# One ScalarE exponential per head in the softmax, in place of GpSimd's subtraction, one wide exponential and VectorE's sums

## Chip, cores and metric

The kernel runs on one core of one Trainium2 chip. The metric is the device time of one execution in microseconds (us). Most executions of one kernel agree within 0.3%.

## What is computed

There are 16 batches of 1024 rows of 512 numbers. Each row attends to the 64 context rows of its batch with 16 heads of 64 numbers each, and a feed-forward part follows. The shapes of the reference, cut to what matters here:

```python
x = x + _L0_xattn_ref(ctx_1024, _layernorm(x, axis=-1), fs, fs, ln1_w, ..., Wq, Wkv, Wout)
...
qk = jnp.einsum('bihd,bjhd->bhij', q, k) * attn_scale
attn = jax.nn.softmax(qk, axis=-1)          # over 64 context rows, for each of 16 heads
out = jnp.einsum('bhij,bjhd->bihd', attn, v)
...
x = x + tanh(layernorm(x) @ weight @ aux_weight1 @ aux_weight2 + bias)
```

## The kernel before

The program has a setup (up to about 150 us), in which weights are split into a high and a low part and multiplied together, and then a loop over 128 tiles of 128 rows. One pass of the loop is called a slot here. Slot t computes the scores and the softmax of tile t, the attention product of tile t-1, and the feed-forward part of tile t-2. Every 32-bit product is three passes on TensorE (PE): high times high, high times low, low times high.

Each engine has its own order of work, written out by hand in `slot_pe`, `slot_act`, `slot_dve`, `slot_pool` and `slot_sp`; each runs in order and waits on semaphores. In a slot PE does:

1. the scores of columns 0 to 511 (half q=0, heads 0 to 7) from xT (L154, L159), the transposes of tile t-2 (L702), the scores of half q=1;
2. the feed-forward product with x2T (L154, L159), which needs ScalarE's x2T_hi (L860) and VectorE's x2T_lo (L944);
3. the attention product of half 0: eight matmuls with pT_hi (L830), which wait for ScalarE's copy (L855), then four with pT_lo (L837), which wait for VectorE's L926; then the same for half 1.

The softmax of one half passes through four engines. VectorE (DVE) scales the scores and adds the bias (L901) and takes the maximum of each head (L906). GpSimd (POOL) subtracts it in two instructions of 256 columns (L994). ScalarE (ACT) takes the exponential of 512 columns in one instruction (L850). DVE sums each head (L912) and inverts the sums (L915). POOL multiplies by the inverse (L1001). SyncE writes the half to DRAM and reads it back rearranged (L752, L759), and in the next slot DVE transposes it (L921, p_turned) and ACT and DVE split it into pT_hi and pT_lo.

ACT's order in an ordinary slot is: x2T_hi, exp(0), pT_hi(0), xT_hi of the next tile (L719), exp(1), pT_hi(1), tanh (L884). DVE's is: x2 (L931), bn_stats, read scores 0, maximum(0), transpose(0), x2T_lo, read scores 1, maximum(1), inverse_sums(0), pT_lo(0), transpose(1), inverse_sums(1), ln1_stats with pT_lo(1) inside it, hid (L977).

Once per batch two slots carry more. Slot m=7 (the last of a batch) folds the next batch's keys into M: 16 pieces on PE (L614, L615), each of which ACT rounds (L632, L633) and DVE and POOL complete (L645, L648, L655), through four PSUM banks; its ACT order is exp(1), pieces 0 and 1, `bias_copy` (L684), pT_hi(1), more pieces. PE does not start the attention product of half 0 there before `s_bs`, the end of `bias_copy`. Slot m=0 folds the values: ACT's `v_prepare_act` (L574) and DVE's `diag_lo` (L557) write bd, then PE makes eight pieces of N from it (L154, L159). There are 15 slots of either kind in the loop, 97 ordinary slots with an attention product, and one slot t=0.

Of the kernel before, what the change touches and what calls it, by code (L numbers as in the profile page):

```python
# [41 lines left out]
ALU = mybir.AluOpType  # L42
ACT = mybir.ActivationFunctionType
AX_XY = mybir.AxisListType.XY

P = 128
# [3 lines left out]
CTX, H, DH = 64, 16, 64  # L50
# [10 lines left out]
def build(nc, x, x_turned, ctx_rows, fs_cols, ln1_w, ln1_b, ln2_w, ln2_b, wqT, wkv, wout, ffn_wT, aux1T, aux2,  # L61
# [7 lines left out]
    with ExitStack() as ctx:  # L69
        def sb(name, cols, dt=F32):  # L70
            return ctx.enter_context(nc.sbuf_tensor(name, [P, cols], dt))

        def sem(name):
            return ctx.enter_context(nc.semaphore(name))
# [26 lines left out]
        mv1, mv2, mv_w = sb("mv1", 2), sb("mv2", 2), sb("mv_w", 8)  # L101
        var1, var2 = sb("var1", 1), sb("var2", 1)
        rs1, rs2 = sb("rs1", 1), sb("rs2", 1)
        row_max = [sb(f"row_max{i}", H) for i in range(2)]
        row_sum = [sb(f"row_sum{i}", H) for i in range(2)]
        row_inv = [sb(f"row_inv{i}", 2 * H) for i in range(2)]

# [19 lines left out]
        S = [take(INNER) for _ in range(2)]  # L127
        xT = [take(D) for _ in range(2)]
        hid = take(D)
        bias = take(INNER)  # L130
# [12 lines left out]
        def at_least(eng, s, n):  # L143

            if not isinstance(n, int) or n > 0:
                eng.wait_ge(s, n)
# [331 lines left out]
        two = lambda name: [sem(f"{name}{i}") for i in range(2)]  # L478
# [5 lines left out]
        s_xT = two("s_xT")  # L484
        s_xTh, s_xTl = sem("s_xTh"), sem("s_xTl")
        s_x2T, s_x2Th, s_x2Tl = sem("s_x2T"), sem("s_x2Th"), sem("s_x2Tl")
        s_sc, s_sb, s_mx, s_sub, s_ex = two("s_sc"), two("s_sb"), two("s_mx"), two("s_sub"), two("s_ex")
        s_sum, s_inv, s_p = two("s_sum"), two("s_inv"), two("s_p")
        s_pw, s_pr = two("s_pw"), two("s_pr")
        s_pt, s_pTh, s_pTl = two("s_pt"), two("s_pTh"), two("s_pTl")  # L490
        s_o, s_x2, s_f, s_fb, s_th, s_y = (sem(n) for n in ("s_o", "s_x2", "s_f", "s_fb", "s_th", "s_y"))
# [8 lines left out]
        J2 = CTX // 2  # L500
        heads = lambda a: a.rearrange("p (h s k j) -> p h k s j", h=2, s=2, j=J2)
        half_of = lambda a, q: a[:, q * BANK:(q + 1) * BANK]
        H2 = H // 2
# [66 lines left out]
        def v_prepare_act(act, b):  # L570
            act.wait_ge(s_vin, 16 * b + 16)
            act.wait_ge(s_m, 16 * b + 16)
            for half in range(2):
                last = act.copy(diag(0, half), dense(kvf, half))  # L574
            last.then_inc(s_vh, 1)
# [92 lines left out]
        def fold_hi(act, b8, cs, produced, done, dst):  # L668
            for c in cs:
                act.wait_ge(produced, b8 + c + 1)  # L670
                act.copy(dst(c), fold_ps[c % 4][:]).then_inc(done, 1)
# [44 lines left out]
        def xT_split_hi(act, u, r):  # L716
            act.wait_ge(s_xT[r], 8 * (u - r) + 16)
            at_least(act, s_sc[1], u)
            act.copy(xT_hi[:], xT[r]).then_inc(s_xTh, 1)  # L719
# [7 lines left out]
        def parts(t, m):  # L727

            known = isinstance(t, int)
            return dict(scores=not known or t < T, following=not known or t + 1 < T,  # L730
                        attn=not known or 1 <= t <= T, chain=not known or t >= 2,
                        fold_m=m == 7 and (not known or t + 1 < T), fold_n=m == 0 and (not known or t < T),
                        more=not known or t + TPB < T)

        def ended(t, m):


            return not isinstance(t, int) or t >= 2
# [104 lines left out]
        def slot_act(act, t, m):  # L843
            has = parts(t, m)
            first = isinstance(t, int) and t == 0

            def exp(q):
                act.wait_ge(s_sub[q], t + 1)
                s = half_of(S[m % 2], q)
                act.activation(s, s, ACT.Exp).then_inc(s_ex[q], 1)  # L850

            def pT_hi_part(q):
                at_least(act, s_o, t - 1)
                act.wait_ge(s_pt[q], t)
                act.copy(half_of(pT_hi, q), half_of(p_turned, q)).then_inc(s_pTh[q], 1)  # L855

            if has["chain"]:
                act.wait_ge(s_x2T, t - 1)
                at_least(act, s_f, t - 2)
                act.copy(x2T_hi[:], x2T_ps[:]).then_inc(s_x2Th, 1)  # L860
            if has["scores"]:
                exp(0)
            if has["attn"]:
                pT_hi_part(0)
            if has["following"]:
                xT_split_hi(act, t + 1, (m + 1) % 2)
            if first:
                fold_hi(act, t, range(6), s_n, s_nh, N_fold[2])
            if has["scores"]:
                exp(1)  # L870
            if has["fold_m"]:
                m_act(act, t + 1, range(2))
                bias_copy(act, t + 1)
            if has["attn"]:
                pT_hi_part(1)
            if has["fold_n"] and not first:
                v_prepare_act(act, t // 8)
            if has["more"] and m == 4:
                k_prepare_act(act, (t + 4) // 8)
            if has["fold_m"]:  # L880
                m_act(act, t + 1, range(2, 10))
            if ended(t, m):
                act.wait_ge(s_fb, t - 1)
                act.activation(hid, hid, ACT.Tanh).then_inc(s_th, 1)  # L884
            if has["fold_m"]:
                m_act(act, t + 1, range(10, 16))
            if has["fold_n"]:
                fold_hi(act, t, range(6 * first, 8), s_n, s_nh, N_fold[2])

        def slot_dve(dve, t, m):  # L890
# [12 lines left out]

            def maximum(q):
                dve.wait_ge(s_sb[q], t + 1)
                dve.tensor_reduce(row_max[m % 2][:, q * H2:(q + 1) * H2], heads(half_of(S[m % 2], q)), AX_XY,  # L906
                                  ALU.max).then_inc(s_mx[q], 1)

            def inverse_sums(q):
                hs = slice(q * H2, (q + 1) * H2)  # L910
                dve.wait_ge(s_ex[q], t + 1)
                dve.tensor_reduce(row_sum[m % 2][:, hs], heads(half_of(S[m % 2], q)), AX_XY, ALU.add).then_inc(s_sum[q], 1)  # L912
                dve.wait_ge(s_sum[q], t + 1)
                sums = row_sum[m % 2][:, hs].rearrange("p (h k) -> p h k", h=2).unsqueeze(2).to_broadcast([P, 2, 2, 4])
                dve.reciprocal(row_inv[m % 2][:, q * H:(q + 1) * H].rearrange("p (h s k) -> p h s k", h=2, s=2),  # L915
                               sums).then_inc(s_inv[q], 1)
# [69 lines left out]
        def slot_pool(pool, t, m):  # L986
            has = parts(t, m)

            def subtract_maximum(q):
                pool.wait_ge(s_mx[q], t + 1)  # L990
                for h in range(2):
                    s = half_of(S[m % 2], q)[:, h * 256:(h + 1) * 256].rearrange("p (s k j) -> p s k j", s=2, j=J2)
                    row = row_max[m % 2][:, q * H2 + 4 * h:q * H2 + 4 * h + 4].unsqueeze(1).unsqueeze(3)
                    last = pool.tensor_tensor(s, s, row.to_broadcast([P, 2, 4, J2]), ALU.subtract)  # L994
                last.then_inc(s_sub[q], 1)

            def normalise(q):
                pool.wait_ge(s_inv[q], t + 1)
                s = half_of(S[m % 2], q).rearrange("p (c j) -> p c j", j=J2)
                inv = row_inv[m % 2][:, q * H:(q + 1) * H].unsqueeze(2).to_broadcast([P, H, J2])  # L1000
                pool.tensor_tensor(s, s, inv, ALU.mult).then_inc(s_p[q], 1)  # L1001

            if has["chain"]:
                pool.wait_ge(s_var2, t - 1)
                at_least(pool, s_fb, t - 2)
                pool.tensor_tensor(rs2[:], var2[:], minus_half[:], ALU.pow).then_inc(s_rs2, 1)  # L1006
            if has["scores"]:
                subtract_maximum(0)
                subtract_maximum(1)
                normalise(0)  # L1010
            if has["fold_m"]:
                m_pool(pool, t + 1, range(1))
            if has["scores"]:
                normalise(1)
            if has["fold_m"]:
                m_pool(pool, t + 1, range(1, 3))
            if has["following"]:
                xT_split_lo(pool, t + 1, (m + 1) % 2)
                pow1(pool, t + 1)
            if has["fold_m"]:  # L1020
                m_pool(pool, t + 1, range(3, 5))
            if ended(t, m):
                pool.wait_ge(s_th, t - 1)
                pool.tensor_tensor(xr[(m - 2) % RING], xr[(m - 2) % RING], hid, ALU.add).then_inc(s_y, 1)
            if has["fold_m"]:
                m_pool(pool, t + 1, range(5, 8))
            if has["more"] and m == 3:
                k_prepare_pool(pool, (t + 5) // 8)
            if has["more"] and m == 4:
                ku_split_lo(pool, (t + 4) // 8)  # L1030
# [86 lines left out]
```

## Time and profile before

| | |
|---|---|
| median of 3 runs | 2230.62 us (2225.62 to 2231.32) |
| the profiled execution, its own time | 2226.84 us |
| its span | 2224.8 us |
| granted TensorE clock, mean | 0.995 of full |
| busy | PE 98%, DVE 82%, POOL 60%, ACT 37% of the span |

Busy shares are averages over the whole span. Whether an engine is in the way is read from what waits for it, and when in a slot.

### The profile page before, as it was taken

To read this page: it belongs to the slowest core of one execution; us is meant where nothing else is said; L and a number is where in the kernel's file an instruction comes from. 1 tells how busy PE (TensorE), PEld (TensorE's weight loads), DVE (VectorE), ACT (ScalarE), POOL (GpSimd) and SP (SyncE) were. 2 spreads that over 40 slices of the span, in tenths; PEclk is the share of its full clock that TensorE was granted. 3 is DMA by queue.
4 is the path that set the end of the run, shared out by engine and by line. 5 is a ranking of instruction groups with operands and counts; after the bars stand their busy time and mean duration, and the time that the engine had idled before them with its cause. 6 is when DMAs were issued, how large, how long until landed. Compare 5 with 4: busy or idle time off the path is not lost.

```text
span 2224.8 us, 34423 instructions
## 1 busy us (share of the span) xinstructions
PE 2169.7 (98%) x10176; PEld 1795.2 (81%) x10176; DVE 1819.1 (82%) x3388; ACT 829.1 (37%) x1623; POOL 1342.2 (60%) x1490
## 2 busy tenths in 40 slices
PE   6999999999999999999999999999999999999998
PEld 5877888888888888888888888888888888878886
DVE  6658888888888888887888888788888888888886
ACT  3353333434333343433334343333434343333422
POOL 4326656575765657575565757556575766657564
PEclk9999999999999999999999999999999999999999
DMA  6434434243433434343342434334243433424342
GB/s 208 158 103 133 121 109 137 95 141 99 127 113 114 131 94 141 99 128 113 115 130 94 141 99 128 112 115 130 94 141 99 129 111 119 131 94 140 96 133 86
DMA packets 284652, 267.19 MB, mean 120 GB/s; under 512 B 61008, under 2 KB 192336, under 8 KB 284624
## 3 DMA queue, kind: packets, MB, share of 16 engines
q1 hardware_dynamic: 284624, 266.84, 38.3%
q8 instruction: 14, 0.23, 0.0%
q14 instruction: 14, 0.11, 0.0%
HBM read 157.68 MB, written 109.05 MB: 120 GB/s over the span
## 4 chain that ended last, share of the span: by engine, by line
PE 81%; DVE 10%; issue 4%; POOL 2%; ACT 1%; DMA 0%; ACTq 0%; SPq 0%; DVEq 0%; POOLq 0%
PE bank L154 34%; PE bank L830 17%; PE bank L159 17%; PE bank L837 9%; PE bank L702 3%; PE bank L614 2%; DVE bd L557 2%; DVE area L645 1%; DVE area L901 1%; DVE row_max L906 1%; DVE bn L691 1%; POOL area L994 1%; DVE p_turned L921 1%; DVE row_sum L912 1%; DVE pT_lo L926 1%
## 5 line engine op out<-in xcount | busy, mean ns | idle before, releaser
L994 POOL TENSOR_TENSOR area<-area,row_max 128x256 f32<-128x256 f32 x512 | 303.9, 615 | 240.9 <-DVE row_max L906 236.2
L154 PE MATMUL bank<-M_hi,xT_hi 128*128 128x512 f32 x1024 | 410.9, 401 | 0.0
L830 PE MATMUL bank<-N_hi,pT_hi 128*128 128x512 f32 x1024 | 402.2, 393 | 0.2
L154 PE MATMUL bank<-M_lo,xT_hi 128*128 128x512 f32 x1024 | 400.7, 391 | 0.0
L830 PE MATMUL bank<-N_lo,pT_hi 128*128 128x512 f32 x1024 | 400.2, 391 | 0.0
L1001 POOL TENSOR_TENSOR area<-area,row_inv 128x512 f32<-128x512 f32 x256 | 326.7, 1276 | 97.2 <-DVE row_inv L915 97.2
L901 DVE SCALAR_TENSOR_TENSOR area<-bank,rs,area 128x512 f32<-128x512 f32 x256 | 192.1, 751 | 176.3 <-PE bank L159 174.2
L850 ACT ACTIVATE area<-area 128x512 f32<-128x512 f32 x256 | 162.1, 633 | 427.1 <-POOL area L994 427.0
L1006 POOL TENSOR_TENSOR rs<-var,minus_half 128x1 f32<-128x1 f32 x128 | 70.5, 551 | 347.8 <-DVE var L698 347.8
L159 PE MATMUL bank<-M_hi,xT_lo 128*128 128x512 f32 x1024 | 274.5, 390 | 3.9 <-POOL xT_lo L724 3.9
L837 PE MATMUL bank<-N_hi,pT_lo 128*128 128x512 f32 x1024 | 276.0, 391 | 1.2 <-DVE pT_lo L926 1.2
L926 DVE TENSOR_TENSOR pT_lo<-p_turned,pT_hi 128x512 fp32r<-128x512 f32 x256 | 262.7, 1026 | 5.4 <-ACT pT_hi L855 1.0
L860 ACT CAST x2T_hi<-bank 128x512 fp32r<-128x512 f32 x128 | 75.2, 587 | 413.7 <-PE bank L702 413.7
L159 PEld LDWEIGHTS bank<-M_hi,xT_lo 128*128 128x128 f32 x1024 | 192.2, 188 | 44.7 <-POOL xT_lo L724 4.3
L830 PEld LDWEIGHTS bank<-N_hi,pT_hi 128*128 128x128 f32 x1024 | 193.4, 189 | 40.3 <-issue 0.5
L830 PEld LDWEIGHTS bank<-N_lo,pT_hi 128*128 128x128 f32 x1024 | 193.4, 189 | 39.4
L154 PEld LDWEIGHTS bank<-M_lo,xT_hi 128*128 128x128 f32 x1024 | 193.3, 189 | 37.1
L154 PEld LDWEIGHTS bank<-M_hi,xT_hi 128*128 128x128 f32 x1024 | 193.0, 188 | 36.2
L837 PEld LDWEIGHTS bank<-N_hi,pT_lo 128*128 128x128 f32 x1024 | 189.8, 188 | 39.5 <-DVE pT_lo L926 1.8
L724 POOL TENSOR_TENSOR xT_lo<-area,xT_hi 128x512 fp32r<-128x512 f32 x127 | 214.6, 1689 | 0.0
L154 PE MATMUL bank<-W_hi,x2T_hi 128*128 128x512 f32 x512 | 199.4, 389 | 1.4 <-ACT x2T_hi L860 1.4
L154 PE MATMUL bank<-W_lo,x2T_hi 128*128 128x512 f32 x512 | 199.2, 389 | 0.0
(127 smaller groups left out, 4123.8 us busy)
## 6 DMA issues: line engine op xcount, KB each, us to landing
p_scratch<-area SPq DMA_DIRECT2D x256, 256.0 KB, 2.0
p_moved<-p_scratch SPq DMA_DIRECT2D x1024, 64.0 KB, 2.1
area<-x_dram SPq DMA_DIRECT2D x128, 256.0 KB, 2.7
area<-x_turned_dram SPq DMA_DIRECT2D x128, 256.0 KB, 2.8
y_dram<-area SPq DMA_DIRECT2D x128, 256.0 KB, 2.1
kv_scratch<-area SPq DMA_DIRECT2D x32, 256.0 KB, 2.4
area<-kv_scratch SPq DMA_DIRECT2D x32, 256.0 KB, 3.6
area<-wkv_dram SPq DMA_DIRECT2D x5, 512.0 KB, 4.5
```

What stands on the lines that cost most here:

```text
L154: mm = eng.matmul(ps, sh, mv, start=(n == 0), stop=False)
L159: mm = eng.matmul(ps, sl, mh, start=False, stop=(k == len(pairs) - 1))
L724: eng.tensor_tensor(xT_lo[:], xT[r], xT_hi[:].bitcast(F32), ALU.subtract).then_inc(s_xTl, 1)
L830: pe.matmul(O_ps[:], pT_hi[:, k * P:(k + 1) * P], n_cols(mv, k), start=(k == 0 and mv is N_hi), stop=False)
L837: mm = pe.matmul(O_ps[:], pT_lo[:, k * P:(k + 1) * P], n_cols(N_hi, k), start=False, stop=(k == 7))
L850: act.activation(s, s, ACT.Exp).then_inc(s_ex[q], 1)
L860: act.copy(x2T_hi[:], x2T_ps[:]).then_inc(s_x2Th, 1)
L901: dve.scalar_tensor_tensor(out=half_of(S[m % 2], q), in0=S_ps[q][:], scalar=rs1[:, 0:1], in1=half_of(bias, q), op0=ALU.mult, op1=ALU.add). ...
L926: dve.tensor_tensor(half_of(pT_lo, q), half_of(p_turned, q), half_of(pT_hi, q).bitcast(F32), ALU.subtract).then_inc(s_pTl[q], 1)
L994: last = pool.tensor_tensor(s, s, row.to_broadcast([P, 2, 4, J2]), ALU.subtract)
L1001: pool.tensor_tensor(s, s, inv, ALU.mult).then_inc(s_p[q], 1)
L1006: pool.tensor_tensor(rs2[:], var2[:], minus_half[:], ALU.pow).then_inc(s_rs2, 1)
```

## The change

The maximum is stored negated. ACT then takes it as its bias, one column for each head, and gives the sum of the exponentials as its accumulated output: eight instructions of 128x64 (2 runs of 32 columns) for each half in place of one of 128x512. GpSimd's subtractions and VectorE's sums are no longer there. Two waits that guard the reuse of `neg_max` and `row_sum` two tiles later are added (`s_inv` on ACT, `s_ex` on DVE); the semaphores `s_sub` and `s_sum` are gone.

```diff
@@ slot_act
             def exp(q):
-                act.wait_ge(s_sub[q], t + 1)
-                s = half_of(S[m % 2], q)
-                act.activation(s, s, ACT.Exp).then_inc(s_ex[q], 1)
+                act.wait_ge(s_mx[q], t + 1)
+                at_least(act, s_inv[q], t - 1)
+                by_head = heads(half_of(S[m % 2], q))
+                for h in range(2):
+                    for k in range(4):
+                        i = q * H2 + 4 * h + k
+                        e = act.activation(by_head[:, h, k], by_head[:, h, k], ACT.Exp, bias=neg_max[m % 2][:, i:i + 1],
+                                           accum_out=row_sum[m % 2][:, i:i + 1])
+                e.then_inc(s_ex[q], 1)
@@ slot_dve
             def maximum(q):
                 dve.wait_ge(s_sb[q], t + 1)
-                dve.tensor_reduce(row_max[m % 2][:, q * H2:(q + 1) * H2], heads(half_of(S[m % 2], q)), AX_XY,
-                                  ALU.max).then_inc(s_mx[q], 1)
+                at_least(dve, s_ex[q], t - 1)
+                dve.tensor_reduce(neg_max[m % 2][:, q * H2:(q + 1) * H2], heads(half_of(S[m % 2], q)), AX_XY,
+                                  ALU.max, negate=True).then_inc(s_mx[q], 1)
 
             def inverse_sums(q):
                 hs = slice(q * H2, (q + 1) * H2)
                 dve.wait_ge(s_ex[q], t + 1)
-                dve.tensor_reduce(row_sum[m % 2][:, hs], heads(half_of(S[m % 2], q)), AX_XY, ALU.add).then_inc(s_sum[q], 1)
-                dve.wait_ge(s_sum[q], t + 1)
@@ slot_pool
-            def subtract_maximum(q):
-                pool.wait_ge(s_mx[q], t + 1)
-                for h in range(2):
-                    s = half_of(S[m % 2], q)[:, h * 256:(h + 1) * 256].rearrange("p (s k j) -> p s k j", s=2, j=J2)
-                    row = row_max[m % 2][:, q * H2 + 4 * h:q * H2 + 4 * h + 4].unsqueeze(1).unsqueeze(3)
-                    last = pool.tensor_tensor(s, s, row.to_broadcast([P, 2, 4, J2]), ALU.subtract)
-                last.then_inc(s_sub[q], 1)
-
...
             if has["scores"]:
-                subtract_maximum(0)
-                subtract_maximum(1)
                 normalise(0)
```

On ACT in a slot m=7, before the change (L719 is xT_hi, L850 exp(1), L632 and L633 the pieces 0 and 1 of M, L684 the four copies of `bias_copy`, L855 is pT_hi(1); `area` holds the scores, `bank` is PSUM):

```order
L719 CAST xT_hi<-area 128x512
L850 ACTIVATE area<-area 128x512
L627 ISA
L632 COPY area<-bank 128x256
L633 CAST M_hi<-bank 128x2x4x32
L627 REGISTER_ALU
L633 CAST M_hi<-bank 128x2x4x32
L684 COPY area<-bank 128x4x2x32 x4
L855 CAST pT_hi<-p_turned 128x512
```

The same place in the changed kernel:

```order
L719 CAST xT_hi<-area 128x512
L854 ACTIVATE area,row_sum<-area,neg_max 128x2x32 x8
L627 ISA
L632 COPY area<-bank 128x256
L633 CAST M_hi<-bank 128x2x4x32
L627 REGISTER_ALU
L633 CAST M_hi<-bank 128x2x4x32
L684 COPY area<-bank 128x4x2x32 x4
L861 CAST pT_hi<-p_turned 128x512
```

Nothing changes its place; the pieces of M, `bias_copy` and pT_hi(1) stand behind eight instructions where they stood behind one.

On DVE in an ordinary slot, before (L906 is the maximum of half 1, L912 and L915 are the sums and their inverses, L926 is pT_lo, L921 the transpose of half 1):

```order
L906 TENSOR_REDUCE row_max<-area 128x8
L912 TENSOR_REDUCE row_sum<-area 128x8
L915 RECIPROCAL row_inv<-row_sum 128x16
L926 TENSOR_TENSOR pT_lo<-p_turned,pT_hi 128x512
L921 STREAM_TRANSPOSE p_turned<-p_moved 128x512
L912 TENSOR_REDUCE row_sum<-area 128x8
L915 RECIPROCAL row_inv<-row_sum 128x16
L691 BN_STATS bn<-area 128x6
```

And in the changed kernel:

```order
L913 TENSOR_REDUCE neg_max<-area 128x8
L920 RECIPROCAL row_inv<-row_sum 128x16
L931 TENSOR_TENSOR pT_lo<-p_turned,pT_hi 128x512
L926 STREAM_TRANSPOSE p_turned<-p_moved 128x512
L920 RECIPROCAL row_inv<-row_sum 128x16
L691 BN_STATS bn<-area 128x6
```

The two sums are gone from their places; the inverses still wait for the exponentials of their half, and what follows on DVE stands behind them as before.

## Rows read from the trace of the kernel before

**Rows 1.** The page, busy time, share of the span and instructions of each engine.

```profile
PE 2169.7 (98%) x10176; PEld 1795.2 (81%) x10176; DVE 1819.1 (82%) x3388; ACT 829.1 (37%) x1623; POOL 1342.2 (60%) x1490
```

**Rows 2.** Windows: slots m=6, 7, 0. Length, then PE, PEld, DVE, ACT, POOL busy.

```profile
880.25:894.32 14.07, 14.07 (x66) 11.65 (x65) 11.42 (x21) 4.14 (x8) 8.95 (x11) 1.00 0.43 132
894.32:918.50 24.18, 23.38 (x134) 19.91 (x133) 19.25 (x43) 12.52 (x36) 14.87 (x19) 1.00 0.36 106
918.50:939.12 20.62, 19.84 (x90) 16.08 (x89) 18.06 (x32) 9.08 (x16) 10.12 (x11) 1.00 0.26 89
```

**Rows 3.** Timeline of PE, slot m=6: attention product, halves 0 and 1. Start, length.

```profile
888.88 0.39 PE L830 MATMUL bank<-N_hi,pT_hi 128*128 128x512 f32 x1
...
891.60 0.39 PE L830 MATMUL bank<-N_hi,pT_hi 128*128 128x512 f32 x1
```

**Rows 4.** Timeline of POOL and DVE, slot m=6.

```profile
884.93 1.19 POOL L994 TENSOR_TENSOR area<-area,row_max 128x256 f32<-128x256 f32 x2
...
884.17 0.68 DVE L906 TENSOR_REDUCE row_max<-area 128x8 f32<-128x512 f32 x1
...
890.86 0.25 DVE L915 RECIPROCAL row_inv<-row_sum 128x16 f32<-128x16 f32 x1
...
891.70 1.09 DVE L926 TENSOR_TENSOR pT_lo<-p_turned,pT_hi 128x512 fp32r<-128x512 f32 x1
```

**Rows 5.** Timeline of ACT, slot m=6.

```profile
886.15 0.63 ACT L850 ACTIVATE area<-area 128x512 f32<-128x512 f32 x1 [1.95 <-POOL area L994]
886.68 0.60 ACT L855 CAST pT_hi<-p_turned 128x512 fp32r<-128x512 f32 x1
887.20 0.62 ACT L719 CAST xT_hi<-area 128x512 fp32r<-128x512 f32 x1
...
890.35 0.62 ACT L855 CAST pT_hi<-p_turned 128x512 fp32r<-128x512 f32 x1 [0.59 <-DVE p_turned L921]
```

**Rows 6.** Groups by line: count, then busy, mean ns of one, idle before.

```profile
L850 ACT ACTIVATE area<-area 128x512 f32<-128x512 f32 x256 | 162.1, 633 | 427.1 <-POOL area L994 427.0
...
L860 ACT CAST x2T_hi<-bank 128x512 fp32r<-128x512 f32 x128 | 75.2, 587 | 413.7 <-PE bank L702 413.7
...
L632 ACT COPY area<-bank 128x256 f32<-128x256 f32 x128 | 47.8, 373 | 64.3 <-POOL M_lo L655 37.3 <-PE bank L615 26.7
```

**Rows 7.** Groups by line, DVE.

```profile
L901 DVE SCALAR_TENSOR_TENSOR area<-bank,rs,area 128x512 f32<-128x512 f32 x256 | 192.1, 751 | 176.3 <-PE bank L159 174.2
...
L931 DVE TENSOR_TENSOR area<-bank,area 128x512 f32<-128x512 f32 x128 | 88.3, 689 | 65.8 <-PE bank L837 65.4
...
L698 DVE TENSOR_SCALAR var<-mv 128x1 f32<-128x1 f32 x256 | 39.5, 154 | 10.1
...
L392 DVE DVE_READ_ACCUMULATOR area<-area 128x1 f32 x6 | 0.5, 81 | 0.0
```

**Rows 8.** Timelines of ACT, DVE and PE, slot m=7.

```profile
903.73 0.35 ACT L632 COPY area<-bank 128x256 f32<-128x256 f32 x1
...
910.28 0.76 DVE L645 TENSOR_TENSOR area<-bank,M_hi 128x256 f32<-128x256 f32 x2
...
906.12 0.45 PE L830 MATMUL bank<-N_hi,pT_hi 128*128 128x512 f32 x1
...
910.83 0.38 PE L614 MATMUL bank<-bd,Wq_hi 128*128 128x256 f32 x1 [0.33 <-DVE area L645]
```

**Rows 9.** Timelines of DVE and PE, slot m=0.

```profile
922.59 0.68 DVE L906 TENSOR_REDUCE row_max<-area 128x8 f32<-128x512 f32 x1
...
929.96 1.09 DVE L926 TENSOR_TENSOR pT_lo<-p_turned,pT_hi 128x512 fp32r<-128x512 f32 x1
...
933.52 0.50 PE L154 MATMUL bank<-Wo_hi,bd 128*128 128x512 f32 x1 [0.78 <-DVE bd L557]
```

**Rows 10.** Windows around a fall of the clock (PEclk is third from last).

```profile
1039.80:1043.20 3.40, 2.70 (x16) 2.26 (x17) 3.30 (x10) 1.54 (x4) 3.14 (x5) 0.94 0.48 128
1043.20:1046.60 3.40, 3.40 (x11) 2.74 (x11) 1.57 (x4) 0.92 (x3) 2.67 (x4) 0.56 0.15 59
```

More of the change, by code:

```diff
@@ L103, in build @@
         rs1, rs2 = sb("rs1", 1), sb("rs2", 1)
-        row_max = [sb(f"row_max{i}", H) for i in range(2)]
+        neg_max = [sb(f"neg_max{i}", H) for i in range(2)]
         row_sum = [sb(f"row_sum{i}", H) for i in range(2)]
@@ L486, in build @@
         s_x2T, s_x2Th, s_x2Tl = sem("s_x2T"), sem("s_x2Th"), sem("s_x2Tl")
-        s_sc, s_sb, s_mx, s_sub, s_ex = two("s_sc"), two("s_sb"), two("s_mx"), two("s_sub"), two("s_ex")
-        s_sum, s_inv, s_p = two("s_sum"), two("s_inv"), two("s_p")
+        s_sc, s_sb, s_mx, s_ex = two("s_sc"), two("s_sb"), two("s_mx"), two("s_ex")
+        s_inv, s_p = two("s_inv"), two("s_p")
         s_pw, s_pr = two("s_pw"), two("s_pr")
```

## The prediction, made before the changed kernel had run

> **What bounds the kernel now.** I read the page's busy times first: PE is busy for 98% of the span, ACT for 37% [rows 1]. So PE sets the time, and the two engines that are relieved, POOL and DVE, can give back only what PE idles for them. The windows by slot show how much that is. An ordinary slot lasts 14.07 us and PE is busy in all of it; PE idles 24.18 - 23.38 = 0.80 us in slot m=7 and 20.62 - 19.84 = 0.78 us in slot m=0 [rows 2]. With 15 batches in the loop, a perfect relief is worth at most 15 x 1.58 = 24 us.
>
> What the change can cost is read from the slack of the work that PE waits for. I count in us from the start of the slot (880.25 for m=6), and read the timelines. PE begins the attention product of half 0 at 8.63 and that of half 1 at 11.35 [rows 3]. They need ACT's pT_hi(0) and pT_hi(1), which stand in ACT's queue behind exp(0) and exp(1). Before, pT_hi(1) begins at 10.10 and ends at 10.72 [rows 5], 0.63 early. No engine's busy share shows this deadline.
>
> **The change, part by part.** Let e be the time from the start of one small exponential to that of the next, its accumulator read included.
>
> *The new time of pT_hi(1), ordinary slot.* The maximum of half 0 ends at 884.17 + 0.68 - 880.25 = 4.60, and its user on POOL begins 0.08 later, at 4.68 [rows 4]. ACT can now begin there. On ACT the copies behind an instruction start 0.53 and 0.52 after it [rows 5], though they last 0.60 and more. So exp(0) holds ACT until 4.68 + 8e, pT_hi(0) and xT_hi until 0.52 x 2 later, exp(1) until 5.72 + 16e; pT_hi(1) ends 0.62 later, and I give 0.07 for the signal to PE (about that from DVE to POOL). PE then has it at 6.41 + 16e. Against 11.35 the stall is **16e - 4.94** where that is positive: the threshold is e = 0.309 us. pT_hi(0) comes at 4.68 + 8e + 0.62 + 0.07 and meets 8.63 up to e = 0.41, so it is not the first to be late.
>
> *What is late next.* DVE's second inverse can start at 5.89 + 16e; the exponential before it ends at 5.82 + 16e, the overlap of 0.10 included. pT_lo(1) starts 891.70 - 890.86 = 0.84 after that inverse and lasts up to 1.09 [rows 4]: 7.82 + 16e. PE wants it eight matmuls (eight of the twelve that fill the 2.72 from half to half, 1.81) after pT_hi(1), at 8.22 + 16e. It keeps 0.3 of slack at any e. The two removed sums lie on DVE, which in an ordinary slot nobody waits for, so they are priced at nothing; so are POOL's subtractions, whose cover is PE's full 14.07 us. If POOL or DVE were the bound they would be worth 2.4 and 1.3 us a slot. The two added waits are for what happened two tiles ago, long past; nothing queues behind them. The DMAs behind POOL's multiplication are issued from the same places.
>
> *The size of e.* No row of the trace shows a 128x64 exponential, a bias column or an accumulator read on ACT. A 512-column exponential takes 633 ns; 587 and 373 ns for 512 and 256 columns from PSUM give 0.836 ns a column [rows 6]. That leaves 205 ns fixed, and 258 ns for 64 columns; less the 0.10 by which the next one overlaps it [rows 5], 0.158. Below this e cannot fall. For the bias column the nearest rows are DVE's: 751 ns with a scalar column against 689 ns without, 62 ns. For the accumulator read it is DVE's own, 81 ns, where a small DVE instruction takes 154 ns [rows 7]. Taken as they stand they give e = 0.301; scaled by the fixed parts of the two engines (205 to 154) they are 83 and 108 ns and e = 0.349. I take **0.33**, between the two. The upper end is that each extra costs a whole fixed part: 0.158 + 2 x 0.205 = 0.568.
>
> The Trainium skill, ScalarE: Activation LUTs, under What ACT_TABLE_LOAD costs, states about 280 ns + 0.833 ns a column with a bias column, and 93 ns of overlap back to back; for 64 columns that is an estimate of 0.240 for the exponential alone, against my 0.220 to 0.241, and it has no price for the accumulator read. This trace has 633 ns for 512 columns without the column, where its rule gives 613. With its 0.240 and my scaled read e would be 0.348, and the sum about 2336 us.
>
> *The sum.* With 16e = 5.28:
> - 97 ordinary slots, 5.28 - 4.94 = 0.34 each: 33 us.
> - Slot m=7: ACT reaches piece 0 of M at 5.72 + 16e; before, it did at 903.73 - 894.32 = 9.41 [rows 8]. So it is 16e - 3.69 = 1.59 late, because before ACT stood idle between its copies and exp(1). Everything behind it moves: `bias_copy` and with it `s_bs`, for which PE holds back half 0 (906.12, no slack but some 0.3); piece 0 of M_hi, then DVE's piece 0, its transpose, pT_hi(1) on ACT, pieces 2 and 3, and DVE's piece 4, for which PE was already waiting (DVE 910.28, PE 910.83 after 0.33 idle [rows 8]). DVE does its steps between without a break, so the 1.6 arrives at PE whole: 15 x 1.6 = 24 us. The saved sum of half 1 does not help there, as DVE waits for ACT at that point.
> - Slot m=0: exp(0) can start at 922.59 + 0.68 + 0.08 - 918.50 = 4.85. That is 0.17 later than in the ordinary slot, so pT_lo(1) starts at 5.89 + 16e + 0.17 + 0.84 = 6.90 + 16e = 12.18, against 929.96 - 918.50 = 11.46; DVE's two writes of bd follow without a gap, and PE was waiting for them already (0.78 idle before 933.52) [rows 9]. So 0.72 more, the slot's own stall included: 15 x 0.72 = 11 us.
>
> Together 68 us. Against the profiled execution's own 2226.8 us that is 2295; that execution was 3.8 us under the median shown, so for a median I say 2230.6 + 68 = **2299 us**, 3% slower. The sum is steep: above the threshold each nanosecond of e is 16 x 127 slots, 2.0 us.
>
> **The rivals.**
> - *The forecast, and the clock falls too.* The trace shows one stretch of 3.4 us with a mean granted clock of 0.56, behind a stretch in which PE was busy for 2.70 of 3.40 us, in a slot m=7 [rows 10]. That is all but wholly the lower of its two levels, 1.2 GHz. Such a stretch loses 3.4 x 0.44 = 1.5 us. Slot m=7 gets 1.6 us more idle time; if this always brings the fall, 15 x 1.5 = 22 us are added: 2321 us. For it: the place is the same. Against it: slots m=0 idle 0.78 at a time at clock 1.00 [rows 2], and the new idle time is spread over several waits.
> - *The accumulator read is a whole instruction on ACT*, 0.205 unoverlapped, with the column at 62 ns: e = 0.425, 16e = 6.80. The ordinary slots stall 1.86, m=7 3.1, m=0 2.2: 180 + 47 + 34 = 261 us, 2492 us. For it: it needs the sum that the exponential before it has just finished. Against it: DVE's costs half of a small instruction of its engine. The skill speaks for this side too: the same page, under Rules for kernel authors, budgets 0.3 us + 0.83 ns a column for every exponential with a bias column, 0.353 for 64 and with DVE's read 0.434, about 2507 us. The rows here show ACT starting the next instruction 0.10 before the last ends [rows 5], which that budget leaves out. At the upper end, e = 0.568, it would be 403 + 82 + 68 = 553 us, 2784 us.
> - *The small exponentials are covered*, e between 0.23 and 0.309: no stall in ordinary slots, only the fold slots pay. At e = 0.301, 16e = 4.82: 17 us for m=7 and 4 for m=0, 2252 us. It is DVE's prices unscaled.
> - *Faster: the relief decides.* Below e = 0.228, where 16e = 3.65, ACT reaches the pieces of M earlier than before and DVE, without 1.3 us of sums, finishes them earlier. At e = 0.158 nearly all of PE's idle time could go: up to 24 us, 2207 us. It needs both extras to be free, or nearly.
>
> **How the numbers follow.** The chances: the forecast 0.40, with the clock 0.15, the dear read 0.22, covered 0.13, faster 0.10. The time is that of the forecast, whose own range, with e from 0.301 to 0.349, is 2252 to 2336. From 2245 to 2490 lie nearly all of the first, second and fourth case and about half of the third, so 8 in 10. 0.3% is 6.7 us, about what a measurement of this kernel can tell from no change: this corresponds to e from 0.21 to 0.255. Most of the last case is beyond it, and a little of the covered one within it: faster 0.07, same 0.07, slower 0.86.
>
> **What would show each step.** The exponentials' group: 2048 instructions and as many accumulator reads, with a start-to-start of 0.33; ACT's busy share up from 37% to about 58% (829 - 162 + 2048 x 0.33 = 1343 us). In an ordinary slot exp(0) starting 4.68 into it and a wait of about 0.3 us of PE L830 for ACT's pT_hi at half 1, none at half 0; the slot 14.4 us. In slot m=7 PE waiting for `bias_copy` and DVE's pieces, the slot near 25.8 us; m=0 near 21.3. No new wait for POOL or a DMA. The prediction is wrong if e is far from 0.33, which is its weakest number, or if PE waits at another place than pT_hi(1).

## The result and the profile after

The changed kernel takes 2311.74 us (median of 4, 2309.98 to 2312.57) against 2229.75 us (4 runs, 2225.62 to 2231.32): ratio 1.037, 95% interval 1.0352 to 1.0388. That is 82 us slower, where 68 were forecast, and 13 us over the predicted 2299.

The page of the changed kernel, its busy times, which answer to [rows 1], then the groups of its longest-running new instructions:

```profile
PE 2214.7 (96%) x10176; PEld 1792.5 (78%) x10176; DVE 1716.7 (74%) x3132; ACT 1349.6 (58%) x5463; POOL 985.5 (43%) x978
...
L854 ACT ACTIVATE area<-area,neg_max 128x64 f32<-128x64 f32 x2048 | 683.5, 335 | 103.3 <-DVE neg_max L913 103.3
...
L854 ACT ACTIVATION_READ_ACCUMULATOR area<-area,neg_max 128x1 f32 x2048 | 383.1, 187 | 0.0
```

ACT went from 37% to 58%, DVE and POOL lost 102 and 357 us of work, and the kernel is slower: none of the four shares says so. What says it is the windows of the same three kinds of slot as in [rows 2], an ordinary one, m=7 and m=0:

```profile
914.35:928.88 14.53, 14.36 (x65) 11.58 (x64) 10.63 (x19) 8.20 (x38) 6.17 (x7) 1.00 0.41 128
928.88:954.67 25.79, 24.02 (x133) 20.16 (x132) 18.34 (x41) 16.76 (x66) 12.18 (x15) 1.00 0.30 99
954.67:975.97 21.30, 20.14 (x89) 16.01 (x88) 17.34 (x30) 13.12 (x46) 7.34 (x7) 1.00 0.26 87
```

The lengths were 14.07, 24.18 and 20.62; they grew by 0.46, 1.61 and 0.68. Where PE waits in the changed kernel, from the view of waits (total, times, longest):

```profile
PE bank L830 <- ACT pT_hi L861: 24.4, 112, 1.3
PE bank L614 <- DVE area L645: 22.5, 45, 0.7
PE bank L154 <- DVE bd L557: 12.5, 15, 0.9
```

The first row is the new one: 112 waits of the attention product for pT_hi, all of them at half 1. One ordinary slot shows it. It starts at 990.50 with PE's first score matmul. The timelines of DVE, ACT and PE:

```profile
994.43 0.69 DVE L913 TENSOR_REDUCE neg_max<-area 128x8 f32<-128x512 f32 x1
...
995.15 0.35 ACT L854 ACTIVATE area<-area,neg_max 128x64 f32<-128x64 f32 x1 [0.71 <-DVE neg_max L913]
995.41 0.19 ACT L854 ACTIVATION_READ_ACCUMULATOR area<-area,neg_max 128x1 f32 x1
995.50 0.34 ACT L854 ACTIVATE area<-area,neg_max 128x64 f32<-128x64 f32 x1
...
999.84 0.70 DVE L926 STREAM_TRANSPOSE p_turned<-p_moved 128x512 f32<-128x512 f32 x1
...
1001.43 0.19 ACT L854 ACTIVATION_READ_ACCUMULATOR area<-area,neg_max 128x1 f32 x1
1001.52 0.60 ACT L861 CAST pT_hi<-p_turned 128x512 fp32r<-128x512 f32 x1
...
1000.94 1.07 PE L837 MATMUL bank<-N_hi,pT_lo 128*128 128x512 f32 x4
1002.18 0.50 PE L830 MATMUL bank<-N_hi,pT_hi 128*128 128x512 f32 x1 [0.17 <-ACT pT_hi L861]
1002.52 0.39 PE L830 MATMUL bank<-N_lo,pT_hi 128*128 128x512 f32 x1
```

Read it against the prediction's walk. exp(0) starts 4.65 into the slot (4.68 forecast). The pair of an exponential and its read repeats every 0.33 us: the read starts 0.24 behind its exponential, the next exponential 0.09 behind the read. pT_hi(1) starts at 11.02, where the walk with e = 0.333 gives 5.72 + 16 x 0.333 = 11.05, right behind the last read. Its input, DVE's transpose, had been done for 1.0 us (at 1000.54), so it is ACT's own queue that held it. PE has pT_hi(1) at 11.68, where it wanted it at 11.35. That is 0.33 of stall by the start times; the row's own 0.17 of idle is less because the profile models the end of the matmul before. The other 0.13 of the slot's 0.46 was not in the sum: after the wait the first matmul runs 0.50, and the second starts 0.34 behind it instead of 0.23.

### The profile page after: what moved, and what is told of

It reads as the page before. It is cut to its first block, busy times and chain, and to the rows that moved or that the text cites. A ratio compares the mean times of both kernels' runs of the same rounds, so it can differ in the third digit from the quotient of the medians.

```text
span 2309.9 us, 37999 instructions
## 1 busy us (share of the span) xinstructions
PE 2214.7 (96%) x10176; PEld 1792.5 (78%) x10176; DVE 1716.7 (74%) x3132; ACT 1349.6 (58%) x5463; POOL 985.5 (43%) x978
## 4 chain that ended last, share of the span: by engine, by line
PE 40%; ACT 36%; DVE 12%; issue 10%; POOL 1%; DMA 0%; DVEq 0%; ACTq 0%; SPq 0%; POOLq 0%
ACT area L854 27%; PE bank L154 15%; PE bank L830 11%; PE bank L159 8%; ACT pT_hi L861 5%; PE bank L837 5%; DVE neg_max L913 4%; ACT xT_hi L719 3%; PE bank L614 2%; DVE bd L557 1%; DVE area L645 1%; DVE mv L695 1%; DVE area L907 1%; DVE bn L691 1%; PE bank L615 0%
## 5 line engine op out<-in xcount | busy, mean ns | idle before, releaser
L854 ACT ACTIVATE area<-area,neg_max 128x64 f32<-128x64 f32 x2048 | 683.5, 335 | 103.3 <-DVE neg_max L913 103.3
L998 POOL TENSOR_TENSOR area<-area,row_inv 128x512 f32<-128x512 f32 x256 | 269.1, 1051 | 726.5 <-DVE row_inv L920 726.5
L830 PE MATMUL bank<-N_hi,pT_hi 128*128 128x512 f32 x1024 | 417.8, 408 | 26.3 <-ACT pT_hi L861 24.4
L854 ACT ACTIVATION_READ_ACCUMULATOR area<-area,neg_max 128x1 f32 x2048 | 383.1, 187 | 0.0
L931 DVE TENSOR_TENSOR pT_lo<-p_turned,pT_hi 128x512 fp32r<-128x512 f32 x256 | 307.7, 1202 | 43.8 <-ACT pT_hi L861 39.4
L890 ACT ACTIVATE area<-area 128x512 f32<-128x512 f32 x128 | 80.9, 632 | 270.0 <-DVE area L982 270.0
```

Of the source, the lines that this page charges most:

```text
L830: pe.matmul(O_ps[:], pT_hi[:, k * P:(k + 1) * P], n_cols(mv, k), start=(k == 0 and mv is N_hi), stop=False)
L854: e = act.activation(by_head[:, h, k], by_head[:, h, k], ACT.Exp, bias=neg_max[m % 2][:, i:i + 1], accum_out=row_sum[m % 2][:, i:i + 1])
L931: dve.tensor_tensor(half_of(pT_lo, q), half_of(p_turned, q), half_of(pT_hi, q).bitcast(F32), ALU.subtract).then_inc(s_pTl[q], 1)
```

## The experiments

The theory is the prediction's: PE waits because pT_hi(1), and in the fold slots other work, stands on ACT behind sixteen small exponentials. The rivals are that each small instruction costs in proportion, that ACT simply has too much work, or that the loss lies elsewhere (DVE's inverses, POOL, the DMAs). Slot lengths below are windows from one slot's first score matmul to the next. Runs 1 to 4 were on one chip, 5 to 8 on a second and 9 and 10 on a third; each group has its own runs of the kernel before (medians 2228.95, 2230.14 and 2228.89 us).

### 1. One more small exponential in each half

```diff
                 by_head = heads(half_of(S[m % 2], q))
+                spare = idle_tile[:, (2 * (m % 2) + q) * 65:(2 * (m % 2) + q + 1) * 65]
+                act.activation(spare[:, 0:64]..., idle_in..., ACT.Exp,
+                               bias=neg_max[m % 2][:, q * H2:q * H2 + 1], accum_out=spare[:, 64:65])
                 for h in range(2):
```

> The changed kernel with a ninth exponential (128x64, bias column, accumulated output) ahead of the eight of each half, on spare tiles; nothing reads it. Theory (the start-to-start time of the small exponentials, 0.333 us, times their number sets when pT_hi(1) reaches PE): 2 x 0.333 = 0.67 us more in every slot with an attention product, ordinary slots 14.53 to 15.20, m=7 and m=0 the same 0.67 longer, 127 x 0.67 = 85 us, 2397 us. Rival (ACT's order is not what PE waits for; the loss comes from DVE's later inverses or from POOL and the DMAs behind them and has slack): clearly less than 85 us, ordinary slots under 14.9.

Measured: 2394.02 us, ratio 1.0743 (1.0725 to 1.0761), 82 us over the changed kernel. The windows:

```profile
940.74:955.97 15.23, 14.43 (x65) 11.58 (x64) 10.70 (x19) 8.88 (x42) 6.18 (x7) 1.00 0.38 122
955.97:982.43 26.46, 24.93 (x133) 21.24 (x132) 18.38 (x41) 17.25 (x70) 12.18 (x15) 0.94 0.32 97
982.43:1004.39 21.96, 20.22 (x90) 15.95 (x88) 17.33 (x30) 13.79 (x50) 7.33 (x7) 1.00 0.25 84
```

Each kind of slot is 0.66 to 0.70 longer than in the changed kernel, where 0.67 was expected. Time on ACT ahead of pT_hi(1) goes one for one into the time of the kernel, in all three kinds. The rival that expects slack falls. The second row has a fall of the clock in it (0.94) and is yet no longer than its like; the last section comes back to it.

### 2. The bias column without the sums

```diff
-                        e = act.activation(..., ACT.Exp, bias=neg_max[m % 2][:, i:i + 1],
-                                           accum_out=row_sum[m % 2][:, i:i + 1])
+                        e = act.activation(..., ACT.Exp, bias=neg_max[m % 2][:, i:i + 1])
@@ inverse_sums
                 dve.wait_ge(s_ex[q], t + 1)
+                dve.tensor_reduce(row_sum[m % 2][:, hs], heads(half_of(S[m % 2], q)), AX_XY, ALU.add).then_inc(s_sum[q], 1)
+                dve.wait_ge(s_sum[q], t + 1)
```

> The changed kernel without the accumulated outputs: sixteen small exponentials with the bias column, DVE's two sums back in their old places, POOL's subtractions still gone. Theory: without its accumulator read an exponential takes 0.24 start to start (the ACTIVATE to its read in the trace of the changed kernel), 16 x 0.24 = 3.84, pT_hi(1) reaches PE at 6.41 + 3.84 = 10.25 of the slot and is covered until 11.35; ordinary slots 14.07, m=7 later by 3.84 - 3.69 = 0.15, sum 2 us: 2232 us, same as before within what can be told. Rival (it is the number of ACT instructions and their waits, not the reads, that costs): ordinary slots stay above 14.3, 2265 us or more.

Measured: 2251.23 us, ratio 1.0107 (1.009 to 1.0123), 19 us more than expected. The windows of an ordinary slot, of m=7, and of the slots m=2 and m=3, then ACT's exp(0) in an ordinary slot:

```profile
890.06:904.13 14.07, 14.07 (x65) 11.66 (x64) 11.17 (x21) 6.83 (x21) 6.46 (x7) 1.00 0.42 131
904.13:928.57 24.44, 23.45 (x133) 19.98 (x132) 18.95 (x43) 15.03 (x49) 12.25 (x14) 1.00 0.33 104
963.17:977.58 14.41, 14.40 (x66) 11.52 (x65) 11.99 (x21) 6.28 (x21) 5.60 (x6) 1.00 0.37 123
977.58:992.28 14.70, 14.31 (x65) 11.59 (x64) 11.09 (x21) 6.77 (x22) 6.53 (x8) 1.00 0.47 145
```

```profile
894.72 2.02 ACT L854 ACTIVATE area<-area,neg_max 128x64 f32<-128x64 f32 x8 [0.71 <-DVE neg_max L912]
896.65 0.60 ACT L860 CAST pT_hi<-p_turned 128x512 fp32r<-128x512 f32 x1
```

The ordinary slot is back at 14.07 with sixteen small exponentials in it: their number is not what costs. Eight of them hold ACT for 1.93 us, 0.24 each, and sixteen stay under the threshold of 4.94. Slot m=7 is 0.26 over before, where 0.15 was expected. The miss is elsewhere. Slot m=2, the last of one pass of the program's loop, is 0.33 longer in every batch, and slot m=3, the first of the next pass, 0.5 to 1.4 longer in the 14 passes that follow another one: some 16 us together. (Expectation 6 below divides this as 1.0 and 0.2; it had set the end of m=2 0.55 too late.) This is DVE at the start of such a slot m=3, which begins at 325.21:

```profile
327.75 0.69 DVE L937 TENSOR_TENSOR area<-bank,area 128x512 f32<-128x512 f32 x1 [2.64 <-issue]
```

DVE's first instruction of the new pass starts 2.54 us into the slot, where it is 0.20 in slots m=3 of the kernel before. DVE is idle for 2.64 us before it, and the release is given as "issue": it waited for nothing that the profile shows. Runs 6, 9 and 10 take this up.

### 3. The same work, with pT_hi(1) ahead of exp(1)

```diff
@@ slot_act
                 pT_hi_part(0)
+                pT_hi_part(1)
...
                 bias_copy(act, t + 1)
-            if has["attn"]:
-                pT_hi_part(1)
@@ slot_dve (behind x2T_lo; then in place of the second transpose and inverse)
+            if has["attn"]:
+                turn_p(1)
...
-                turn_p(1)
-            if has["scores"]:
-                inverse_sums(1)
+                pT_lo_part(1)
...
-                ln1_stats(dve, t + 1, (m + 1) % RING, (lambda: pT_lo_part(1)) if has["attn"] else None)
+                ln1_stats(dve, t + 1, (m + 1) % RING, (lambda: inverse_sums(1)) if has["scores"] else None)
```

> The changed kernel with the same instructions in another order: on ACT pT_hi(1) ahead of xT_hi and exp(1), on DVE the second transpose behind x2T_lo, pT_lo(1) ahead of ln1_stats, the second inverse inside ln1_stats. Theory (PE waits because pT_hi(1) stands behind exp(1)): ordinary slots 14.07 again, though ACT does as much as in the changed kernel; m=0 about 0.25 over its 20.61 of before; m=7 still late, as the pieces of M and bias_copy stand behind exp(1): 1.4 over 24.20. 2230 + 25 = 2254 us. Rival (ACT has too much work in a slot, wherever it stands): slots stay near 14.5, 2300 us or more.

Measured: 2257.59 us, ratio 1.0127 (1.011 to 1.0144). The windows of an ordinary slot, m=7 and m=0, and ACT's timeline in the ordinary one:

```profile
893.40:907.47 14.07, 14.07 (x65) 11.65 (x64) 10.22 (x19) 8.21 (x37) 5.85 (x7) 1.00 0.45 133
907.47:932.63 25.16, 23.30 (x134) 20.05 (x133) 18.64 (x41) 16.19 (x65) 12.68 (x16) 1.00 0.35 114
932.63:953.78 21.15, 19.82 (x89) 16.07 (x88) 17.26 (x30) 13.12 (x46) 7.31 (x7) 1.00 0.27 87
```

```profile
900.73 1.13 ACT L861 CAST pT_hi<-p_turned 128x512 fp32r<-128x512 f32 x2
```

ACT is busy for 8.21 us of the ordinary slot, as in the changed kernel (8.20), and PE for all of it. Both copies are done 1.1 us after the last exponential of exp(0), at 901.86, and PE wants the second only at 904.75. So ACT does not have too much work; the place in its queue was the fault. The edit moves DVE's steps too, so run 3 alone does not separate ACT's queue from DVE's; the timeline above does, with the transpose done 1.0 us before ACT came to it. What is left of the loss lies in the fold slots, +0.98 and +0.53 (expected 1.4 and 0.25), and some 7 us in slots m=3.

### 4. The sums without the bias column

```diff
 # in the kernel before, GpSimd's subtractions kept
-                act.activation(s, s, ACT.Exp).then_inc(s_ex[q], 1)
...
+                for h in range(2):
+                    for k in range(4):
+                        i = q * H2 + 4 * h + k
+                        e = act.activation(by_head[:, h, k], by_head[:, h, k], ACT.Exp,
+                                           accum_out=row_sum[m % 2][:, i:i + 1])
+                e.then_inc(s_ex[q], 1)
 # DVE's two sums are gone, as in the change
```

> The kernel before with the single wide exponential cut into eight of 128x64 with accumulated outputs and no bias column; POOL's subtractions stay, DVE's sums are gone. One look, for the price of the bias column: theory, start to start 0.158 + 0.093 for the read = 0.25 us against 0.333 with the column, so the column costs 0.08; pT_hi(1) reaches PE 0.3 to 0.4 late, as exp(0) starts only behind POOL's subtraction; about 2300 us. Rival: the column is hidden when the instructions stand back to back, start to start 0.33 here too, and the time then is near 2400 us.

Measured, one run and so without an interval: 2287.49 us, with ordinary slots of 14.36. Its groups by line, and ACT's timeline:

```profile
L854 ACT ACTIVATE area<-area 128x64 f32<-128x64 f32 x2048 | 494.5, 243 | 262.7 <-POOL area L998 262.6
L854 ACT ACTIVATION_READ_ACCUMULATOR area<-area 128x1 f32 x2048 | 383.3, 187 | 0.0
```

```profile
1001.45 0.24 ACT L854 ACTIVATE area<-area 128x64 f32<-128x64 f32 x1
1001.60 0.19 ACT L854 ACTIVATION_READ_ACCUMULATOR area<-area 128x1 f32 x1
1001.69 0.24 ACT L854 ACTIVATE area<-area 128x64 f32<-128x64 f32 x1
```

Without the column an exponential and its read take 0.24 start to start, with it 0.33; one exponential lasts 243 ns and 335 ns. So the column costs 0.09, and it is not hidden back to back. The read costs 0.09 as well, since run 2 has 0.24 with the column and without the read. The three prices of the prediction's e were 0.158 for the bare exponential, about 0.07 for the column and about 0.09 for the read; they are 0.15, 0.09 and 0.09. The 0.15 is what is left of 0.333; no run has the bare exponential back to back.

### 5. Half 0 changed, half 1 as before

```diff
             def exp(q):
+                if q == 1:
+                    act.wait_ge(s_sub1, t + 1)
+                    s = half_of(S[m % 2], q)
+                    act.activation(s, s, ACT.Exp).then_inc(s_ex[q], 1)
+                    return
...
             def inverse_sums(q):
+                if q == 1:
+                    dve.tensor_reduce(row_sum..., ALU.add).then_inc(s_sum1, 1)
...
 # maximum(1) is not negated; subtract_maximum, as before, is back in slot_pool
@@ slot_pool
+                subtract_maximum(1)
                 normalise(0)
```

> Half 0 as in the changed kernel (eight exponentials with bias column and sums), half 1 as before (GpSimd's subtraction, one wide exponential, VectorE's sum). Theory (the threshold: ACT may spend 4.94 us of a slot on exponentials before PE waits for pT_hi(1)): exp(0) takes 8 x 0.333 = 2.66, exp(1) starts behind POOL's subtraction at about 8.93 of the slot (8.88 before), so ordinary slots are 14.07, m=7 within 0.1 of 24.20; 2230 us, same as before within what can be told, and half of the change costs nothing rather than half of 82 us. Rival (each small exponential costs its share): 2270 us. An added wait where the loop begins again, as in the bias-only kernel, could add up to 15 us.

Measured: 2263.97 us, ratio 1.0159 (1.0128 to 1.0191). The expected 2230 is missed by 34 us, and the rival's 2270 is near; the total alone would have chosen wrongly. The ordinary slots are 14.07, as the theory has it. The windows of m=7 and m=3, and ACT's exp(1) and piece 0 of M in the m=7:

```profile
905.70:930.34 24.64, 23.75 (x133) 20.06 (x132) 18.52 (x42) 14.75 (x51) 13.78 (x17) 1.00 0.34 105
979.26:994.72 15.46, 14.43 (x66) 11.51 (x64) 10.82 (x20) 6.67 (x23) 7.77 (x9) 1.00 0.46 137
```

```profile
915.03 0.63 ACT L854 ACTIVATE area<-area 128x512 f32<-128x512 f32 x1 [0.87 <-POOL area L1009]
915.57 0.35 ACT L633 COPY area<-bank 128x256 f32<-128x256 f32 x1
```

m=7 was expected within 0.1 of before and is 0.46 over, 7 us in all: exp(1) waits there for POOL's subtraction and starts at 9.33 where 8.93 was expected, so ACT reaches piece 0 of M 9.87 into the slot, 0.46 later than before (9.41). The slots m=3, with the late start of DVE again, give some 24 us. That was allowed for with up to 15 us, which was too little.

### 6, 9 and 10. Twenty-four small instructions ahead of the loop

```diff
@@ setup_dve, in the kernels of run 2, of the change itself, and of run 7
+            for n in range(24):
+                dve.memset(idle_in[:, n:n + 1], 0.0)
```

> The bias-only kernel with 24 more memsets of 128x1 on VectorE in the setup, nothing in the loop changed. Its question: the bias-only kernel lost 1.0 us in slots m=2 and 0.2 in slots m=3, where the loop begins again and VectorE's x2 started 2.6 us late with nothing to wait for. Theory (it depends on where the loop's instructions lie): the loss at the loop's start changes, most likely goes, and 2251 us becomes about 2235 us. Rival (it belongs to the loop's own work, more ACT instructions in one pass): the same slots lose the same, 2251 us.

> The changed kernel with 24 memsets of 128x1 more on VectorE in the setup, nothing in the loop changed. In the changed kernel VectorE does not start late where the loop begins again; in the bias-only kernel it did, and the same 24 memsets cut that from up to 3.3 to 2.7 us and took away what PE lost by it. Theory (it depends on where VectorE's instructions lie in memory): a late start of x2 with nothing to wait for can appear here, 14 times, worth 0 to 1 us each: 2312 to 2326 us, and the reason for the 82 us stays pT_hi(1) either way, ordinary slots 14.53. Rival (the late start belongs to the order of VectorE's loop, not to its place): 2312 us, no such start.

> The kernel with the fold slots reordered and the same 24 memsets. Theory (place): the 0.22 us that slots m=2 and m=3 lose each go, 14 x 0.44 = 6 us, 2200 us. Rival: the same 2205.6 us.

In these expectations too, what is put down to slots m=2 in runs 2 and 7 lies for the greater part in slots m=3. Measured: the bias-only kernel falls from 2251.23 to 2232.68 us (ratio to before 1.0013, 1.0003 to 1.0022), which is the 2232 that run 2 expected. The changed kernel rises from 2311.74 to 2325.72 us (1.0435, 1.0418 to 1.0453). The kernel of run 7 falls from 2205.62 to 2200.47 us (0.9873, 0.9856 to 0.9889). None of them has a changed instruction in its loop. The windows of the shifted changed kernel, an ordinary slot and the m=3 at the loop's edge, and its waits of DVE (total, times, longest):

```profile
1325.83:1340.38 14.55, 14.40 (x65) 11.57 (x64) 10.65 (x19) 8.20 (x38) 6.15 (x7) 1.00 0.41 127
1416.55:1432.10 15.55, 14.77 (x65) 11.41 (x64) 10.63 (x19) 8.21 (x38) 6.17 (x7) 1.00 0.47 136
```

```profile
DVE area L939 <- issue: 37.1, 14, 2.8
```

So instructions that run once, ahead of the loop, decide whether the late start is there and how long it is. That what matters is where DVE's code lies is the likely reading; no run shows it. It happens 14 times, as often as the loop starts again. What it costs depends on when DVE's x2 starts in slot m=3 (us from the slot's start; it is 0.20 in the kernel before and in the changed one):

| | x2 starts at | slot m=3 is longer by |
|---|---|---|
| run 6, bias only, shifted | 1.8 to 2.0 | 0 to 0.2 |
| run 9, the change, shifted | 2.1 to 2.4 | 0.8 to 1.1 |
| run 2, bias only | 2.3 to 3.2 | 0.5 to 1.4 |
| run 5, one half | 3.1 to 3.7 | 1.4 to 2.0 |

The page's queue of instructions (q14) has 88 packets in the changed kernel and 158 in the shifted one. That is 70 more, as many as 5 for each of the 14 restarts. But the count alone does not go with the late start. The kernel before has 14 and no late start, the changed kernel and run 1 have 88 and 103 and none either, and runs 2, 5 and 6 have 86 each with starts from 1.8 to 3.7 us into the slot. That a reload of instructions is the cause, of which engine's, and what decides whether it is needed, stays open.

### 7 and 8. The fold slots reordered too, with and without the change

```diff
@@ slot_act, on top of run 3 (run 8: the same order in the kernel before)
             if has["fold_m"]:
                 m_act(act, t + 1, range(2))
                 bias_copy(act, t + 1)
+                m_act(act, t + 1, range(2, 4))
             if has["fold_n"] and not first:
                 v_prepare_act(act, t // 8)
+            if has["scores"]:
+                exp(1)
@@ slot_dve: diag_lo of bd ahead of ln1_stats; slot_pool: m_pool of pair 1 ahead of normalise(1)
```

> The reordered kernel (pT_hi(1) ahead of exp(1)) in which, in slots m=7 and m=0, also the pieces 0 to 3 of M and bias_copy, and v_prepare_act and VectorE's bd, stand ahead of exp(1). Theory (what is left of the loss is the same queueing behind the small exponentials in the fold slots): m=7 falls from 25.17 to about 23.7 (0.5 under before, as PE idles less), m=0 from 21.17 to about 19.85 (no wait for bd), ordinary 14.07; 2257.6 - 22 - 20 = 2216 us, 0.6% faster than before. Rival (in the fold slots DVE's own chain is the bound, which the order on ACT does not change): m=7 stays over 24.2, 2235 us or more.

> The kernel before (subtraction on GpSimd, one wide exponential, sums on VectorE) with the same reordering as the last one. It tells whether a gain there comes from the exponentials with bias and sum or from the order alone. Theory: from the order alone; m=0 19.9 as v_prepare_act and bd are ahead, m=7 within 0.3 of the last kernel's, 2210 to 2220 us. Rival (VectorE's two sums, 1.3 us, and GpSimd's subtractions are what m=7 needs off): m=7 24.0 or more and 8 us or more slower than the last one.

Measured: 2205.62 us (ratio 0.9893, 0.9876 to 0.9909) with the change and 2209.34 us (0.9912, 0.9896 to 0.9929) without it. The windows of the first, ordinary slot, m=7, m=0, then m=7 and m=0 of the second:

```profile
875.10:889.17 14.07, 14.07 (x65) 11.66 (x64) 10.22 (x19) 8.21 (x37) 5.84 (x7) 1.00 0.41 133
889.17:912.67 23.50, 23.06 (x133) 20.00 (x132) 18.59 (x41) 16.21 (x65) 12.74 (x16) 1.00 0.38 122
912.67:932.18 19.51, 19.51 (x89) 16.16 (x88) 16.37 (x30) 13.36 (x46) 6.41 (x7) 1.00 0.23 78
```

```profile
1147.04:1170.12 23.08, 22.90 (x133) 19.92 (x132) 19.23 (x43) 12.60 (x36) 16.33 (x20) 1.00 0.39 125
913.77:933.73 19.96, 19.82 (x90) 16.08 (x89) 17.56 (x32) 8.77 (x16) 9.19 (x11) 1.00 0.21 73
```

With the change m=7 is 0.68 and m=0 is 1.11 shorter than before, more than expected (0.5 and 0.75), and the total is 10 us under the expected 2216. Nearly all of the gain is the order's: the kernel before, in the same order, has 21 of the 25 us, and run 8's rival, that m=7 needs the sums and subtractions off DVE and POOL, falls with 23.08. In this order the change makes m=0 0.45 shorter and m=7 0.42 longer. The total is 3.7 us lower with it, each of its runs under each of the others, but each also loses some 7 us in one ordinary slot a batch (m=3 with the change, where DVE starts late again; m=5 without it, not traced), so what the change itself is worth is open. With the 24 memsets the changed one takes 2200.47 us, 1.3% under the kernel before; the other was not run with them.

## Why the prediction came out right

- **The bound.** "PE sets the time" held, and so did the threshold of 16e = 4.94 as far as the runs can tell: 3.9 us of exponentials on ACT cost an ordinary slot nothing (run 2), 5.33 us stall PE for 0.33. The stall came where the walk put it, at pT_hi(1), with none at pT_hi(0).
- **The size of e.** 0.33 was taken and 0.333 measured. Its parts were less good, as run 4 shows; the column came out dearer than DVE's 62 ns. The two errors, 0.158 for 0.15 and the column, nearly cancelled. That a value chosen in the middle between 0.301 and 0.349 came within 4 ns is in part luck: at the sum's 2.0 us a nanosecond those ends are 2252 and 2336 us.
- **The Trainium skill.** The Trainium skill, ScalarE: Activation LUTs, under What ACT_TABLE_LOAD costs, gives 93 ns for a column operand and 93 ns of overlap back to back; worked out from its figures, an exponential of 64 columns with the column is an estimate of 0.240 us start to start. The traces agree, with 335 ns (the changed kernel) against 243 (run 4), and 0.24 start to start in run 2. The Trainium skill's budget on the same page, under Rules for kernel authors, about 0.3 us and 0.83 ns a column, which the prediction weighed as a rival, does not hold back to back, by the same 0.24. (The prediction's "about 2507" for it is 2510 by its own sum.)
- **Ordinary slots** are the term that was mis-sized: 0.34 each, 33 us, against 0.46 (0.53 in slots m=3), 46 us for 95 of them. The stall itself was 0.33, about as forecast: e's 0.003 more, times 16, was met by as much that came earlier than in the walk. What was missing is the 0.13 that PE took to come back to its spacing after the wait, which had no price in the sum.
- **Slot m=7**: 1.6 forecast, 1.61 measured. Its steps can be followed. ACT reaches piece 0 of M at 939.90, 11.02 into the slot (11.00 forecast), and DVE reaches piece 4 at 946.44, 17.56 (15.96 before, and 1.59), before PE's wait at 946.99. DVE does not work there without a break, as the prediction has it: it stands idle for 1.15 us before piece 2, until ACT has rounded it (0.43 before the change). The delay reaches it through ACT all the same.

```profile
939.90 0.35 ACT L632 COPY area<-bank 128x256 f32<-128x256 f32 x1
...
943.67 0.76 DVE L645 TENSOR_TENSOR area<-bank,M_hi 128x256 f32<-128x256 f32 x2 [1.15 <-ACT M_hi L633]
...
946.44 0.76 DVE L645 TENSOR_TENSOR area<-bank,M_hi 128x256 f32<-128x256 f32 x2
...
946.99 0.38 PE L614 MATMUL bank<-bd,Wq_hi 128*128 128x256 f32 x1 [0.40 <-DVE area L645]
```

- **Slot m=0**: 0.72 forecast, 0.68 measured.
- **What was not in it.** The spans of the two profiled executions differ by 85.1 us: 46 in ordinary slots, 24 in m=7 and 10 in m=0, 3 in the slots t=0 and t=1, and 1.6 for one more fall of the clock (below). The median of before was also 1 us lower in the new runs.
- **The rivals.** A fall of the clock in every m=7 did not come. It came in 3 of 15, against 2 of 15 before. Its premise is not empty, though: in run 1, where PE waits longer still, the clock fell in 10 of 15. The dear read, the covered case and the faster case are excluded by e itself.

## What to carry to other kernels

Before a long instruction on a half-idle engine is cut into many short ones, look for what stands behind it in that engine's queue and when its reader wants it: here 4.94 us of a 14 us slot were free (3.69 in slot m=7), and the 5.33 that were used cost the whole kernel 3.7%, while the engine was 58% busy. Price a small instruction by its start-to-start time, the operand column and the read each on its own. Before a change is given up, try the order: the same work in another place was 1.1% faster than the kernel before. And judge an edit by the slots that it touches, since code elsewhere moved the total by 5 to 20 us.

## What the runs showed of the hardware that was not expected

- On ACT an accumulator read lasts 187 ns but holds up the next exponential by 0.09 us. A bias column adds 0.09 us to a 128x64 exponential, back to back too.
- After a wait of 0.33 us PE took some 0.1 us more to come back to its spacing: 0.34 from the first matmul to the second, then 0.23.
- DVE's first instruction of a pass of the loop can start 1.6 to 3.5 us later than in the kernel before (runs 2, 5, 6 and 9), waiting for nothing that the profile shows; 24 small instructions ahead of the loop moved three kernels by -19, +14 and -5 us.
- Before and in the changed kernel, the slots m=7 in which the granted clock fell to its lower level, 1.2 GHz, for a while are 1.6 us longer than their like; it fell on the product of half 1 in all five. This one, of the changed kernel, is 27.38 against 25.79:

```profile
792.86:820.24 27.38, 25.63 (x133) 21.27 (x132) 18.34 (x41) 16.77 (x66) 12.17 (x15) 0.94 0.32 102
810.60:814.00 3.40, 2.54 (x17) 2.11 (x17) 3.33 (x9) 1.53 (x4) 2.99 (x4) 1.00 0.38 96
814.00:817.40 3.40, 3.40 (x10) 2.70 (x10) 1.69 (x5) 0.92 (x3) 2.81 (x4) 0.50 0.11 42
```

- Where a fall lay decided what it cost. In run 1 the clock fell in ten slots m=7, and nine of them are no longer than the rest (26.4 to 26.5). In those nine it fell on the product of half 0, ahead of waits for DVE's pieces that took up the loss; in the tenth it fell on the product of half 1, and that slot is 28.0. One of the nine:

```profile
966.60:970.00 3.40, 1.91 (x14) 1.59 (x13) 1.65 (x4) 3.02 (x15) 0.74 (x1) 1.00 0.03 9
970.00:973.40 3.40, 3.40 (x11) 2.72 (x10) 2.18 (x7) 1.99 (x6) 1.79 (x2) 0.51 0.26 89
```
